# Log attention in one TensorE pass over values and ones side by side, with the rows picked apart once a batch

## What is computed

```python
L = einsum('bhqd,bhkd->bhqk', q, k) * scale
L_y = einsum('bhqd,bhkd->bhqk', q, k_y) * scale
agg = sum(exp(clip(L_y, -15, 15)) * mask, axis=-1, keepdims=True) + EPS
r = log(abs(L) + EPS) - log(agg + EPS)
w = softplus(r) * mask
A = w / (sum(w, axis=-1, keepdims=True) + EPS)
out = einsum('bhqk,bhkd->bhqd', A, v)
```

## Time and profile before

| | us |
|---|---|
| median of 3 runs | 1077.15 |
| lowest, highest | 1073.49, 1079.67 |
| span of the profiled execution | 1063.2 |
| TensorE busy | 851.5 |
| VectorE busy | 739.8 |
| ScalarE busy | 565.3 |
| GpSimd busy | 549.6 |

### The profile page before, as it was taken

One profiled execution on the slowest core, in us unless ns is written; L12 is line 12 of the kernel. 1 busy time (PEld: TensorE's weight loads), 2 busy tenths in 40 slices (PEclk: granted clock), 3 DMA queues, 4 the chain that ended last, 5 costly groups with the idle time before them and its releaser, 6 DMA issues.

```text
span 1063.2 us, 21402 instructions
## 1 busy us (share of the span) xinstructions
PE 851.5 (80%) x7419; PEld 570.4 (54%) x7419; DVE 739.8 (70%) x1570; ACT 565.3 (53%) x797; POOL 549.6 (52%) x758
## 2 busy tenths in 40 slices
PE   4777477899985768888878888889888767899890
PEld 3666466799972333333333333333444346799890
DVE  4988845465564569798878887788878835455574
ACT  2444152233345679787877888788763332233230
POOL 1111385880555655666533333333413787788784
PEclk9989678999996899999999999999877788999896
DMA  9970012133346756564736263632210021132434
GB/s 294 273 104 2 15 38 70 61 98 101 106 116 177 223 166 191 158 186 144 197 100 199 85 207 107 195 105 61 80 40 11 31 77 40 39 91 81 138 119 132
DMA packets 114120, 123.84 MB, mean 116 GB/s; under 512 B 13297, under 2 KB 76273, under 8 KB 113889
## 3 DMA queue, kind: packets, MB, share of 16 engines
q1 hardware_dynamic: 96224, 100.54, 33.9%
q0 software_dynamic: 8416, 17.29, 5.2%
q10 hardware_dynamic: 9376, 4.65, 1.5%
HBM read 59.71 MB, written 62.72 MB: 115 GB/s over the span
## 4 chain that ended last, share of the span: by engine, by line
PE 45%; DVE 18%; issue 14%; POOL 9%; DMA 6%; ACT 5%; SPq 3%; DVEq 0%; POOLq 0%; ACTq 0%
PE psum L1775 7%; PE psum L820 7%; PE psum L1727 5%; DVE ring_b L1993 4%; PE psum L1759 4%; PE psum L834 4%; POOL x_sorted L1033 3%; POOL y_token L1057 2%; PE psum L1793 2%; POOL pause_room L478 2%; PE psum L772 2%; PE psum L783 2%; DVE parts L2000 2%; PE psum L743 2%; SPq L2141 1%
## 5 line engine op out<-in xcount | busy, mean ns | idle before, releaser
L1993 DVE TENSOR_SCALAR ring_b<-psum 128x1024 int32<-128x1024 int32 x160 | 195.0, 1222 | 66.4 <-PE psum L1727 65.6
L1867 ACT ACTIVATE ring_a<-psum 128x1024 f32<-128x1024 f32 x160 | 163.1, 1024 | 82.7 <-PE psum L1727 79.1
L2104 POOL TENSOR_SCALAR_AFFINE_SELECT ring_b<-ring_b 128x512 f32<-128x512 f32 (+1 forms) x112 | 84.7, 770 | 213.6 <-ACT ring_b L1873 213.4
L1873 ACT ACTIVATE ring_b<-ring_b 128x1024 f32<-128x1024 f32 x160 | 168.4, 1053 | 41.5 <-DVE ring_b L1993 41.1
L1985 DVE TENSOR_SCALAR ring_a<-ring_a 128x1024 f32<-128x1024 f32 x160 | 120.9, 760 | 22.3 <-ACT ring_a L1867 22.3
L1727 PE MATMUL psum<-stacks 32*128 32x128 f32 (+3 forms) x1024 | 102.3, 384 | 41.2 <-DVE ring_b L1993 21.9
L1727 PEld LDWEIGHTS psum<-stacks 32*128 32x128 f32 x1024 | 58.8, 191 | 131.3 <-issue 74.8
L935 ACT ACTIVATE ring_b<-psum 128x512 f32<-128x512 f32 x72 | 42.6, 591 | 112.8 <-PE psum L820 79.3
L1775 PE MATMUL psum<-ring_b,values 128*32 128x256 f32 (+3 forms) x1024 | 89.9, 460 | 9.1 <-POOL ring_b L2104 5.6
L2104 POOL TENSOR_SCALAR_AFFINE_SELECT ring_a<-ring_a 128x512 f32<-128x512 f32 (+1 forms) x112 | 81.2, 738 | 27.0 <-DVE ring_a L1985 26.9
L1078 POOL DMA_INDIRECT r_rows<-y_sorted,rows_of x64 | 69.5, 1086 | 49.3 <-DMA y_sorted<-y_out 36.9
(11 more groups left out here) (211 smaller groups left out, 1478.6 us busy)
## 6 DMA issues: line engine op xcount, KB each, us to landing
stack_q<-parts SPq DMA_DIRECT2D x32, 256.0 KB
stack_ky<-parts SPq DMA_DIRECT2D x32, 256.0 KB
stacks<-stack_q SPq DMA_DIRECT2D x64, 128.0 KB
stacks<-stack_ky SPq DMA_DIRECT2D x64, 128.0 KB
stack_k<-parts SPq DMA_DIRECT2D x32, 256.0 KB
stacks<-stack_k SPq DMA_DIRECT2D x64, 128.0 KB
stack_qr<-parts SPq DMA_DIRECT2D x32, 256.0 KB
stacks<-stack_qr SPq DMA_DIRECT2D x64, 128.0 KB
```

The costliest lines, as they stand in the source:

```text
L1867: nc.scalar.activation(exps[:, n % RING, 2 * u:2 * u + 2, :], psum[:, first:first + 2, :], ACT.Exp, scale=SCALE).then_inc(self.exp, 1)
L1873: nc.scalar.activation(part, part, ACT.Ln, bias=1.0).then_inc(self.ln, 1)
L1993: nc.vector.tensor_scalar(ring[:, m % RING, HEADS_B[u][0]:HEADS_B[u][1] + 1, :].bitcast(I32), psum[:, first:first + 2, :].bitcast(I32), 0x ...
L2104: ins = nc.gpsimd.affine_select(out=part, in_=part, pattern=[[0, part.ap[1][1]], [1, 128]], compare_op=ALU.is_ge, fill=0.0, base=0, channe ...
```

## The change

The weights of a head's values were 32 columns, of which eight at the head's own place hold the values and the others are zero. Now heads of one group share a bank only in pairs: a head's 32 columns hold, at 0 or 16 by the head's parity, eight values and eight ones beside them. One pass gives numerators and sums in interleaved rows. Heads 0 and 1 of each group go to bank 5 and are complete after five steps, heads 2 and 3 go to bank 6; `PIECES` is reordered for that. The pass stands behind u = 1 in every step. Once a batch, ScalarE copies bank 5 out (i = 3) and VectorE bank 6 (i = 8), into two rooms that are free then, and TensorE picks the sums (end of i = 8) and the numerators (end of i = 9) out of both with constant 0/1 matrices, two matmuls of 128x512 each, into bank 6. VectorE adds the correction to the sums at i = 9 and to the numerators at i = 0; `correct` moves from the end of i = 9 to i = 0, behind the absolute values of u = 1, and `divide` from i = 9 to i = 0. The ones are set by a second memset on GpSimd, and the two constants of 128 KB are loaded.

```diff
+    for name, shift in (("pick_numerators", 0), ("pick_sums", HD)):
+        pick = np.zeros((128, 2, D))
+        pick[32 * group + 2 * HD * (stack % 2) + shift + dim, stack // 2, column] = 1
...
                     nc.gpsimd.memset(values[:], 0.0).then_inc(set_values, 1)
+                    p.wait_ge(set_values, 1)
+                    ones = bass.AP(values, HD, [values[:].ap[0], [2 * OW, 2 * TT * HALF], [OW + 2 * HD, 2], [1, HD]])
+                    nc.gpsimd.memset(ones, 1.0).then_inc(set_values, 1)
...
-                  [(0, 2, 0, 256, 256), (1, 2, 256, 256, 256)], [(2, 2, 0, 256, 256), (3, 2, 256, 256, 256)],
-                  [(2, 1, 0, 128, 384), (2, 3, 384, 384, 128)], [(2, 0, 0, 0, 512)],
+                  [(0, 2, 0, 256, 256), (1, 2, 256, 256, 256)], [(2, 0, 0, 0, 512)],
+                  [(2, 1, 0, 128, 384), (2, 3, 384, 384, 128)], [(2, 2, 0, 256, 256), (3, 2, 256, 256, 256)],
...
+        FULL = {0: 5, 5: 6}
+        HALF_DONE = 5
+        evicted = q_scaled, r_buf[:]
...
-            def weight_values(self, pe, m, into):
+            def weight_values(self, pe, m):
...
+                pe.wait_ge(self.mask_b, m + 1)
+                if i == 0:
+                    pe.wait_ge(self.v_ready, b + 1)
+                    pe.wait_ge(self.first_out, b)
+                if i == HALF_DONE:
+                    pe.wait_ge(self.emptied, 2 * b)
+                into = 5 if i < HALF_DONE else 6
...
+            def pick(self, pe, b, n):
+                if n == 0:
+                    pe.wait_ge(self.first_out, b + 1)
+                    pe.wait_ge(self.second_out, b + 1)
+                else:
+                    pe.wait_ge(self.emptied, 2 * b + 1)
+                for a in range(2):
+                    mm = nc.tensor.matmul(bank(6), picks[n][:, a, :], evicted[a], start=a == 0, stop=a == 1)
+                mm.then_inc(self.picked, 1)
...
-                first_of_batch = (m - 2) % DUS == 0
-                if 0 <= m - 2 < STEPS_A and not first_of_batch:
-                    self.weight_values(pe, m - 2, 5)
...
                 if 0 <= m - 2 < STEPS_A:
-                    if first_of_batch:
-                        self.weight_values(pe, m - 2, 5)
-                    self.weight_values(pe, m - 2, 6)
+                    self.weight_values(pe, m - 2)
+                if i in (8, 9) and 0 <= a - 2 < B:
+                    self.pick(pe, a - 2, i - 8)
...
+            def evict_first(self, a, b):
+                a.wait_ge(self.weighted, DUS * b + HALF_DONE)
+                if b + 1 < B:
+                    a.wait_ge(self.low, SPLITS.index(("qr", b + 1)) + 1)
+                nc.scalar.copy(evicted[0], bank(5)).then_inc(self.first_out, 1)
...
-                if i == 8 and 0 <= a - 2 < B:
+                if i == 9 and 0 <= a - 2 < B:
                     self.invert_weights(a_, a - 2)
...
+            def evict_second(self, v, b):
                 v.wait_ge(self.weighted, DUS * (b + 1))
+                v.wait_ge(self.q_ready, min(b + 2, B))
+                nc.vector.tensor_copy(evicted[1], bank(6)).then_inc(self.second_out, 1)
...
+                nc.vector.tensor_tensor(d_buf[:], bank(6), delta_n, ALU.add).then_inc(self.emptied, 1)
...
+                nc.vector.tensor_tensor(oT[:], bank(6), delta_v, ALU.add).then_inc(self.emptied, 1)
...
                 if i == 8 and 0 <= a - 2 < B:
-                    self.empty(v, a - 2)
+                    self.evict_second(v, a - 2)
+                if i == 9 and 0 <= a - 2 < B:
+                    self.take_sums(v, a - 2)
+                if i == 0 and 0 <= a - 3 < B:
+                    self.take_numerators(v, a - 3)
...
+                if i == 0 and 0 <= a - 2 < B:
+                    self.correct(v, a - 2)
...
-                if i == 9 and 0 <= a - 2 < B:
-                    self.divide(v, a - 2)
-                if i == 9 and 0 <= a - 1 < B:
-                    self.correct(v, a - 1)
+                if i == 0 and 0 <= a - 3 < B:
+                    self.divide(v, a - 3)
...
                     self.vector_step(v, n)
+                self.take_numerators(v, B - 1)
+                self.divide(v, B - 1)
```

More of the change, by code:

```diff
@@ L78, in shape_constants @@
     tables["empty_rows"] = 1 + 2 * B * T + np.arange(4 * QUADS)[None, :] * 128 + np.arange(128)[:, None]
+    column = np.arange(D)
+    group, stack, dim = column // 32, column // HD % GROUPS, column % HD
+    for name, shift in (("pick_numerators", 0), ("pick_sums", HD)):
+        pick = np.zeros((128, 2, D))
+        pick[32 * group + 2 * HD * (stack % 2) + shift + dim, stack // 2, column] = 1
+        tables[name] = pick
     tables["choice_rank"] = np.tile(np.arange(ROUTED, 0, -1, dtype=np.float32), (128, 1))
@@ L1607, in build @@
         delta = sb("delta", [128, T])
+        evicted = q_scaled, r_buf[:]
+        picks = [const[k][:].rearrange("p (a n) -> p a n", a=2) for k in ("pick_sums", "pick_numerators")]
         delta_v, delta_n = (y_out[:, k].rearrange("p s n -> p (s n)") for k in range(2))
@@ L1762, in sum_exps @@
                 mm.then_inc(self.sums, 1)
-            def weight_values(self, pe, m, into):
+            def weight_values(self, pe, m):
                 b, i = divmod(m, DUS)
[L1767 to L1771, removed]
+                pe.wait_ge(self.mask_b, m + 1)
[5 more added lines that the diff above has]
+                into = 5 if i < HALF_DONE else 6
                 for s, kb, column, q0, width in PIECES[i]:
                     for j in range(4):
-                        weight = values[:, b % 2, kb, 4 * j + s, :] if into == 5 else ones_s[:, s, :]
-                        mm = nc.tensor.matmul(psum[32 * j:32 * j + 32, into, q0:q0 + width], weight,
-                                              ring[:, m % RING, j, column:column + width], start=i == 0,
-                                              stop=i == DUS - 1, skip_group_check=True, tile_position=(0, 32 * j))
-                if into == 6:
-                    mm.then_inc(self.weighted, 1)
+                        mm = nc.tensor.matmul(psum[32 * j:32 * j + 32, into, q0:q0 + width], values[:, b % 2, kb, 4 * j + s, :],
+                                              ring[:, m % RING, j, column:column + width], start=FULL.get(i) == into,
+                                              stop=i in (HALF_DONE - 1, DUS - 1), skip_group_check=True,
+                                              tile_position=(0, 32 * j))
+                mm.then_inc(self.weighted, 1)
+            def pick(self, pe, b, n):
[7 more added lines that the diff above has]
+                mm.then_inc(self.picked, 1)
             def turn(self, pe, b):
@@ L1939, in scalar_step @@
                     self.copy_xT(a_, a + 1)
+                if i == 3 and 0 <= a - 2 < B:
+                    self.evict_first(a_, a - 2)
                 if i in (4, 5, 6) and 0 <= a + 1 < B:
```

37 lines of the change are left out of this document (24 added, 13 removed).

## The result

The changed kernel's median is 1087.9 us (1080.13 to 1088.45, 4 runs); before, beside it, 1075.32 us (1070.92 to 1079.67, 4 runs). The ratio is 1.0129, 95% interval [1.0092, 1.0166]: slower, by 10 to 18 us. The prediction was 1087 us, +10.

The account below looks back on a forecast made before the run. The path was taken to alternate between TensorE and VectorE, with most of the removed pass cover. Steady +6.6, head -2, tail +3.5 and clock +2 sum to +10 us, on a median of 1077.15: 1087 us, range 1074 to 1100.

Parts of the forecast that it names:

- Most of the 91.6 us is cover: Ones pass on TensorE: most of its 91.6 us busy time only covers waits, as the path alternates with VectorE.
- The rival in which TensorE sets the pace: Each of 80 steps would save 0.98 us; about -45 us in all, 1032 us; chance 0.03.
- The floor of 2.03 us from u0 to u1: Between a step's two score blocks (halves of the heads): at least 2.03 us, as VectorE's absolute values free the bank.
- The -0.27: First halves of steps 2, 3, 5, 6 and 7: 2.30 falls to 2.03 us each, -1.35 per batch.
- Picks: Ends of steps 8 and 9: 2.1 us each, unhidden; the steps become 6.41 (+0.60) and 6.42 us (+1.83).
- Moved correction: Step 0: the q2 projection waits for the correction on VectorE; step goes from 6.03 to 6.38 us, +0.35.
- Steady sum: Net of the step terms: +1.43 us per batch, +6.6 over the five full batches (steps 28 to 77).
- Clock: TensorE's granted clock drops after new gaps, about 1.7 us a drop: +2 us, from 0 to +8.
- the rival that the clock falls in every batch: Drops in every batch and more low stretches in the tail: about +12 us more, 1099 us; chance 0.11.
- Head: Steps 18 to 27: no picks yet, one pass less and shorter first halves; -2 us, from -2.5 to 0.
- Tail: Steps 78 to 99 and the end, with picks, fewer passes and late evictions: +3.5 us, from -3 to +9.
- that ring of waits: Tail, from step 83: chain from score block through VectorE to router logits, about 6.7 us whatever TensorE does; -1.3 over steps 84 to 87.

Follow-up runs that it names:

- e5: The kernel before, without the ones pass in eight of a batch's ten units, most sums left out; 1096.48 us, ratio 1.0227.
- e12: e5 with the pass put back over zero weights in six of the eight units, sums still left out; 1069.8 us, ratio 0.9989.
- e2: The changed kernel with the numerators' pick cut to 64 of 512 columns; 1083.4 us, ratio to before 1.0087.
- e6: The changed kernel with both evictions and both pick matrices in bfloat16; 1082.0 us, ratio to before 1.0098.
- e3: The changed kernel with the correction back at the end of step 9, its product in two alternating rooms; 1087.98 us, ratio to before 1.0163.
- e8: The changed kernel with a zero-weight pass added ahead of the weighting pass in steps 0, 1, 2, 4, 5 and 6; 1079.54 us, ratio to before 1.0077.
- e9: e7 with the zero-weight passes of e8 added; 1064.23 us, ratio to before 0.9947.
- e7: The changed kernel with the edits of e6 and e3 together; 1071.66 us, ratio to before 1.0006.
- e11: The kernel before with two more useless matmuls ahead of the router logits in each of steps 83 to 86; ratio 1.0.

## Why the prediction came out right, step by step

- *Most of the 91.6 us is cover.* Right, and too weak: e5 and e12 show that taking eight tenths of the pass away without anything else costs 2.3%, and zeros in its place bring the time back. The rival in which TensorE sets the pace is refuted: e5 takes out the work almost alone, and gets slower.
- *The floor of 2.03 us from u0 to u1.* Right: 2.02 to 2.09 in all steps of these two batches but 1 and 4 in the first (2.54 and 3.17) and 2 in the second (2.59, at the low clock). The -0.27 were -0.20 to -0.27, in steps 3, 5, 6 and 7. Step 2 still ends in a wait for VectorE (2.06 us for L2096) and gains nothing; step 4 gained 0.24 or, by its longer values, lost 0.18.
- *Picks.* Mis-sized: 2.1 us a pair by the q projection's row, 1.82 measured (587.22 to 589.04, and 593.31 to 595.13). The row that I took ended at a score block; behind a pick another 128x128 product follows, and it starts 0.96 or 0.86 us after it. The prefix behind them was priced 0.1 too dear in the same way (0.73 and 0.74 measured). Steps 8 and 9 became 6.02 and 6.10 us, not 6.41 and 6.42. My estimate from the four passes of which the Trainium skill speaks (FP8 and Floating Point Precision, the part on FP32) was 0.85 us for one such matmul, and the trace has 0.91 for one of two: nearer than my 1.05. e2 and e6 shorten steps 8 and 9, but their whole gain isn't clear of noise, as step 0 takes much of it back.
- *Moved correction.* Right: q2 waits for it (1.82 us), step 0 went from 6.03 to 6.46, forecast 6.38. e3 shows that undoing it alone moves the loss into step 1, where the clock falls.
- *Steady sum.* +1.43 a batch were +1.1 or +1.5, by the value taken for step 4. Over steps 28 to 77 I had +6.6 and most of the +2 for the clock; measured +8.7 in one profile of each, of which 5 to 7 are the steps.
- *Clock.* The direction was right, the mechanism only in part, and how much of the loss it has isn't well known. I counted gaps and a price for each, and not the removed work. In the one profile it has the other 2 to 4 us of the stretch. By e8, zero passes won 5.6 us (1.0129 to 1.0077, two sets of runs, 1 to 10 us by the intervals), so +2 is likely too little. The 8.2 us that are left in e8 are near the forecast without its clock term, 6.6 - 2 + 3.5 = 8.1; the zero passes may have had a cost or a use of their own. The condition of the rival that the clock falls in every batch came true: steps at the low clock in five batches of five against two, eight falls in 410 to 700 us against two, 15 waits of over 1.5 us against 8. Its price didn't: 12 us more by 1.7 us a fall, where the whole stretch got 8.7 longer, steps included. A fall can be made good by a later wait: the changed kernel's second batch in the table has two starred steps and is its shortest full one, with a step 4 of 5.58 us. The rule of the Trainium skill (TensorE: Matmul & The Clock Gate, Part 1), that the gate follows how busy the engine has recently been, agrees with the table: e5 and e12 do the same but for useless work, and have .89 and .98.
- *Head.* Wrong: -2 forecast, but from the first score block of step 18 to that of step 28 it was 55.29 us before (399.18 to 454.47) and 55.44 after (409.47 to 464.91). Step 18 did fall, by 1.0 (5.30 to 4.30; -0.9 forecast), but step 19 gave 0.8 of it back (4.61 to 5.39) at the full clock: VectorE is behind, and u1 waits 1.38 us for it (416.87) and follows u0 after 3.10 us, above the floor of 2.03. The clock has a part too: before has 1.00 there (401 to 457 us), after .94 (410 to 467), and e9, which has the same pass and a clock of 1.00, takes 54.1 us. I counted work removed, and neither VectorE's queue behind it nor the clock that it had held.
- *Tail.* +3.5 forecast, +4.1 measured, in other places. At the first router logits it was +3.8 (+2.6 forecast for steps 78 to 82: 29.14 and 32.90 us after step 78's first score block). The -1.3 over steps 84 to 87 did not come: from the first logits to the sixth it was -0.3 (35.38 to 35.05). I had that ring of waits going on "whatever TensorE does", but the logits and scores in it are TensorE's, and it takes 7.5 us at the low clock and 6.4 at the full one. At the last pass it was +3.4 (1.5 forecast), and the end gave +0.7 instead of +2.
- *From sum to time.* +10 against +12.6 [9.9 to 17.9]. From step 18 to the last shared down products the profiles differ by 12.9 us, where my terms gave 10.1: the head has 2.1 of the difference, the tail 0.6, and in the steady part steps somewhat too dear stand against a clock too cheap. Some of the closeness of 1087 to 1087.9 is luck: the prediction stood on a median of 1077.15 for the kernel before, and with a fourth run that is 1075.32; from there, +10 is 1085.3. The 13.95 us between span and median play no part, since they put the span back to the median.

Not settled: why e3 and e6 add up so well in e7 beyond steps 8 to 0, and how much of the 12.6 us the clock has in an average execution; each profile is one execution.

## What to carry to other kernels

Before counting a removed pass as a gain, look at what ends the wait behind it: if another engine does, the pass was cover, and on TensorE cover can also hold the clock (e5 against e12), so that removing it can cost more than it weighs. Shorten the chain that the waits end on first (here the picks and the correction, e7), then give TensorE something to do in the gaps that are left (e9), and follow the gain to the end: in the tail such a filler took 3.5 us off a row of steps, and another engine's queue behind them took it back (e11). Price an operation behind another of its kind by the distance of their starts, and compare kernels by marks inside the profile, not by one span against a median.

## What the runs showed that I had not expected

- Leaving out 73 us of TensorE's work cost 24 us (e5), and matmuls over zero weights brought them back (e12: 0.9989).
- The clock fell after waits of 1.67 us here (623.00), and with no wait of over 1 us just before it there: in the changed kernel's first batches a projection took 1.88 us instead of 1.12 behind a wait of 0.94:

```profile
450.69 1.07 PE L1792 MATMUL psum<-ring_b,values 128*32 128x256 f32 x16
452.70 1.88 PE L1821 MATMUL psum<-o_tok,b_k 128*128 128x512 f32 x2 [0.94 <-DVE parts L2035]
```

- Two edits that alone were within noise of nothing (-3 and +4 us) were worth -13 us together (e6, e3, e7), since each alone leaves the other's wait at the end of the chain.
- In the tail, the clock at which eight small matmuls run (1.84 or 1.03 us) sets whether a step takes 7.5 or 6.4 us, while sixteen larger ones beside them can run at either without a change.
- In bfloat16 a pick's matmul is one record of 0.39 us, and two of them take 0.44 us from start to start of what follows; in float32 it is two records, together 1.13 us, and the next starts 0.96 us behind.
